# A gated delta-rule layer with experts on one core: the first inverse level begins its banks, and three VectorE instructions of each item go to ScalarE and GpSimd

## The chip, the cores and the metric

The kernel runs on one core of one Trainium2 chip. The metric is the device time of one execution, in microseconds. A core has TensorE (matrix products, in the rows PE, its weight loads PEld), VectorE (DVE), ScalarE (ACT), GpSimd (POOL) and SyncE (SP), which issues the DMAs. Each engine works through its own list of instructions in order; semaphores tie the lists together.

## The reference, cut to what matters

One layer over 2 sequences of 2048 tokens with 256 features: a gated delta-rule attention (16 value heads and 8 key heads of 128), and behind it a mixture of 16 experts. The part that the change touches:

```python
mixed = hidden_states @ Wqkv.T + bqkv          # then a causal convolution of 4 taps along the tokens, and silu
q = _l2norm(q) * DK ** (-0.5); k = _l2norm(k)   # _l2norm(x) = x * rsqrt(sum(x * x) + 1e-6)
def step(state, inp):                           # for every token
    state = state * jnp.exp(g_t)[..., None, None]
    delta = (v_t - jnp.einsum('bhk,bhkv->bhv', k_t, state)) * b_t[..., None]
    state = state + k_t[..., None] * delta[:, :, None, :]
    out = jnp.einsum('bhk,bhkv->bhv', q_t, state)
var = jnp.mean(core * core, axis=-1, keepdims=True)
core = core * lax.rsqrt(var + RMS_EPS) * norm_w * jax.nn.silu(zg)
```

## The kernel before

The tokens are cut into 32 chunks of 128, and the 16 value heads into 4 groups of 4. One **item** is one group g of one chunk t; g is also called its slot. The recurrence inside a chunk is solved in matrix form, which needs the inverse of a 128x128 unit triangular matrix for each head. GpSimd inverts the 16x16 blocks on the diagonal (`base_inverse`); SyncE takes the triangle `Ln` to DRAM and the blocks back, and then the block inverses to DRAM and into the full tiles `XiT` and `Xi`. TensorE then doubles the block size in three levels.

The work is pipelined over items by hand. In each engine's `item(w, stages)` five items are in flight: `a` (three ahead: projection, convolution taps, gate), `f` (two ahead: norms, exponents, the triangle), `v` (one ahead: the inverse levels), `w` (the state's recurrence) and `u` (one behind: output projection). The order of calls in `item` is the order on the engine; nothing else decides it. The experts of chunk t-1 and the front of chunk t+1 are laid in at fixed slots.

A level n of the inverse is: TensorE `invert_q` (L554: bQ = LnR applied to XiT), VectorE `mask_q` (L1191: Qi = bQ times the level's 0/1 mask), TensorE `invert_xt` (L562, into bank bXT) and `invert_x` (L567, into bank bX), ScalarE `inverse_t` and `inverse` (L934 and L941, which copy the banks back to XiT and Xi). The banks accumulate: `invert_begin` first puts XiT and Xi themselves into them by a product with the identity (L544, L545), and each level adds its correction. After the third level TensorE turns XiT (`turned`, L573), forms the residual (L580, L582), and in the next item corrects Xi (`correct`, L589), which VectorE copies to Tt (`refined`, L1207). Tt is what the state's solve (L611) multiplies with.

Other lines that the steps touch:
- TensorE: `kkq` and `exponents` (L526 to L530, with bf16 products), `ss` (L501: row sums of the squares of q and k, it waits for ScalarE's Sq, L880), `z_proj` (L484, L486).
- VectorE: `taps` (L1148), `tails_out` (L1162, needs Bk and Hd), `first_tokens` (L1172), `squares` (L1183 makes Sse = sum + epsilon, L1185 makes Epq from it), `ended` (L1154 makes Bk, the bias of the rows that end a sequence), `out_norm` (L1237 sums ScalarE's squares of O along the row into Ss, L1239 makes Vv), `gate_bias` (L1201).
- ScalarE: `square_o` (L959, squares O into CoT), `activated` (a table load, three Silus, a table load, Sq), `key_norm` (L897), `out_norm` (L963, L965), `norm` (L975, L977), `decays` (L925, makes Ex).
- GpSimd: `exponents` (HG and Parts), `before_first` (L1495 to L1501, makes Hd), `decay_keys` (Kd), `minus_l` and `attention` (L1481), `base_inverse` (L1577 to L1604).

Of the kernel before, what the change touches and what calls it, by code (L numbers as in the profile page):

```python
# [35 lines left out]
ALU = mybir.AluOpType  # L36
# [3 lines left out]
P = 128  # L40
# [29 lines left out]
def constants(chunks, chunks_of_batch):  # L70
# [8 lines left out]
    for n in range(LEVELS):  # L79
        b = r >> (LO + n)  # L80
        f[:, C_LEVEL + n * P:C_LEVEL + (n + 1) * P] = (b[:, None] % 2 == 1) & (b[None, :] == b[:, None] - 1)
    last = np.arange(chunks) % chunks_of_batch == chunks_of_batch - 1
# [18 lines left out]
def layer_kernel(nc, x, wqkv, conv, wz, wba, rows, cols, wout, shared1, wlat, shared2, wup, rw, rw2,  # L101
# [6 lines left out]
    with ctx:  # L108
# [64 lines left out]
        Sse = sb("Sse", [P, 2 * GK])  # L173
        Epq = sb("Epq", [P, GROUPS, GK])
# [70 lines left out]
        def heads(bank):  # L245
# [12 lines left out]
            xt_done=LEVELS, sq_done=1, lnr_done=1, oq_done=1,  # L258

            bk_done=1, tails_done=2, convqk_done=TAPS, convv_done=TAPS, sse_done=1, epq_done=1, kkq_done=1, hg_done=4, parts_done=5,  # L260
            q_done=LEVELS + 1, tt_done=1, r_done=2, o_done=2, s_done=2, so_done=1, vv_done=1, core_done=1, acc_done=1,

            h_done=5, neg_done=1, at_done=1, kd_done=2, base_done=BASE_STEPS,
# [187 lines left out]
        def _(pe):  # L451
# [81 lines left out]
            def invert_begin(v, front):  # L533
                f = ahead(v, 1)
                if front:
                    pe.wait_ge(sem["partsT_done"], at("partsT_done", f))
                    pe.wait_ge(sem["vs_done"], at("vs_done", f))
                    pe.wait_ge(sem["ex_done"], at("ex_done", f))
                else:
                    pe.wait_ge(sem["xt_done"], at("xt_done", ahead(v, -1)))  # L540
                    pe.wait_ge(sem["tt_done"], at("tt_done", ahead(v, -1)))
                    pe.wait_ge(sem["q_done"], at("q_done", ahead(v, -1)))
                pe.wait_ge(sem["xb_in"], at("xb_in", v))
                mm(bXT[:, :], IdR[:, 0, :], XiT[:, :, :], start=True, stop=True)  # L544
                mm(bX[:, :], IdR[:, 0, :], Xi[:, :, :], start=True, stop=True)  # L545

            def invert_q(v, n):
                if n == 0:
                    pe.wait_ge(sem["lnr_done"], at("lnr_done", v))
                else:  # L550
                    pe.wait_ge(sem["xt_done"], at("xt_done", v, n))
                    pe.wait_ge(sem["q_done"], at("q_done", v, n))
                for h in range(GH):
                    last = mm(heads(bQ)[:, h, :], LnR[:, h, :], XiT[:, h, :], start=True, stop=True)  # L554
                last.then_inc(sem["q_full"], 1)

            def invert_xt(v, n):
# [1120 lines left out]
```

## Time and profile before

| what | value |
|---|---|
| median of 3 runs | 3390.93 us (3383.54 to 3395.1) |
| the profiled execution | 3389.08 us, its span 3387.3 us |
| granted TensorE clock, mean | 0.988 |
| TensorE busy | 3222.1 us, 95% |
| its weight loads | 2861.1 us, 84% |
| VectorE busy | 2720.6 us, 80% |
| ScalarE busy | 2412.1 us, 71% |
| GpSimd busy | 2140.9 us, 63% |
| DMA | 15.8% of 16 engines' span |

The busy share of every engine is the same in each fortieth of the span but the first and the last, so one chunk stands for all. In the chunk that the rows below are from, slot 0 starts at 1516.78 us, slot 1 at 1540.63, slot 2 at 1568.20 and slot 3 at 1594.17, by the first product of the state (L603) on TensorE. A timeline merges equal instructions that follow one another: its second column then runs from the first one's start to the last one's end. TensorE's ends are modelled, and a product is recorded as longer than the distance to the next one's start, so its price in the stream is read from start to start.

### The profile page before, as it was taken

What the parts mean: (1) busy time and instruction counts of PE and PEld (TensorE: products, weight loads), DVE (VectorE), ACT (ScalarE), POOL (GpSimd) and SP (SyncE); (2) the same over time, 40 slices, a digit from 0 to 9 for tenths busy, and PEclk for the clock granted to TensorE, in tenths of its full rate; (3) what the DMA queues carried; (4) which work ended last, traced back from release to release, by engine and by line L of the source; (5) the groups of instructions that cost most, each with busy time, mean ns of one, the idle gap of its engine ahead of it and who ended that gap; (6) DMA issues with size and microseconds to landing.
All of it is one profiled execution on the core that took longest, in us unless ns stands there. A gap on an engine that the chain in (4) does not pass through costs nothing.

```text
span 3387.3 us, 77356 instructions
## 1 busy us (share of the span) xinstructions
PE 3222.1 (95%) x24096; PEld 2861.1 (84%) x24096; DVE 2720.6 (80%) x8720; ACT 2412.1 (71%) x5922; POOL 2140.9 (63%) x5380
## 2 busy tenths in 40 slices
PE   4999999999999999999999999999999999999996
PEld 3888888888888888888888888888888888888885
DVE  4788888888888888888888878888888888888874
ACT  3777777777777777777777777777777777777762
POOL 2766666666666666666666666666666666666660
PEclk8999999999999999999999999999999999999997
DMA  4111111111111111111111111111111111111110
GB/s 181 36 46 38 37 44 38 38 44 41 36 43 40 38 44 41 36 40 42 37 39 47 36 35 45 40 38 44 40 34 45 41 37 45 39 34 43 43 36 11
DMA packets 424114, 144.77 MB, mean 43 GB/s; under 512 B 211168, under 2 KB 421664, under 8 KB 423200
## 3 DMA queue, kind: packets, MB, share of 16 engines
q1 hardware_dynamic: 423712, 139.83, 15.8%
q8 instruction: 201, 3.29, 0.4%
q14 instruction: 201, 1.65, 0.2%
HBM read 93.11 MB, written 46.66 MB: 41 GB/s over the span
## 4 chain that ended last, share of the span: by engine, by line
PE 64%; ACT 12%; DVE 9%; issue 8%; POOL 4%; DMA 3%; SPq 0%; DVEq 0%; ACTq 0%; POOLq 0%
PE bF L473 8%; PE bB L644 6%; PE bQ L554 4%; ACT L847 4%; PE bS L611 3%; PE bXT L562 3%; PE bB L729 3%; PE bB L716 3%; PE bXT L501 2%; PE bS L619 2%; PE bD L626 2%; PE bQ L493 2%; PE bS L603 2%; PE bF L484 2%; PE bD L604 2%
## 5 line engine op out<-in xcount | busy, mean ns | idle before, releaser
L1148 DVE SCALAR_TENSOR_TENSOR Y<-bF,Cv,Y 128x127 f32<-128x127 f32 (+2 forms) x3072 | 850.8, 338 | 7.2 <-ACT Y L864 2.4
L473 PE MATMUL bF<-XnT,Wqkv 128*128 128x128 f32 x4096 | 533.5, 278 | 0.5 <-ACT XnT L983 0.5
L473 PEld LDWEIGHTS bF<-XnT,Wqkv 128*128 128x128 f32 x4096 | 507.0, 194 | 9.5 <-issue 2.1
L864 ACT ACTIVATE Y<-bF,Cv 128x128 f32<-128x128 f32 x1024 | 382.6, 454 | 102.1 <-PE bF L473 102.1
L934 ACT ACTIVATE XiT<-bXT 128x512 fp32r<-128x512 f32 x384 | 228.7, 596 | 307.2 <-PE bXT L562 302.4
L1587 POOL TENSOR_TENSOR Tp<-Tp 32x64 f32<-32x64 f32 (+2 forms) x768 | 360.0, 469 | 60.2
L1191 DVE TENSOR_TENSOR Qi<-bQ,Cf 128x512 fp32r<-128x512 f32 x384 | 263.6, 686 | 99.2 <-PE bQ L554 97.8
L847 ACT ACT_TABLE_LOAD x257 | 329.7, 1283 | 5.3 <-PEq L1671 0.7
L562 PE MATMUL bXT<-Qi,Xi 128*128 128x128 f32 x1536 | 302.5, 320 | 2.3 <-DVE Qi L1191 2.3
L562 PEld LDWEIGHTS bXT<-Qi,Xi 128*128 128x128 f32 x1536 | 222.6, 192 | 96.4 <-DVE Qi L1191 46.3
L1580 POOL TENSOR_TENSOR Tp<-Yb,Tm 32x64 f32<-32x64 f32 (+1 forms) x384 | 276.6, 720 | 30.1
L1580 POOL TENSOR_TENSOR Tp<-Cb,Yb 32x64 f32<-32x64 f32 (+1 forms) x384 | 274.0, 713 | 30.1
L1595 POOL TENSOR_TENSOR Yb<-Cb,Cf 32x8 fp32r<-32x8 f32 x128 | 25.7, 201 | 410.8 <-DMA Cb<-DL 410.8
L554 PE MATMUL bQ<-XiT,LnR 128*128 128x128 f32 x1536 | 240.9, 280 | 19.4 <-ACT XiT L934 19.4
L554 PEld LDWEIGHTS bQ<-XiT,LnR 128*128 128x128 f32 x1536 | 211.9, 191 | 47.9 <-ACT XiT L934 28.8
L644 PE MATMUL bB<-Wout,CoT 128*128 128x256 f32 x1024 | 244.2, 382 | 0.9 <-ACT CoT L970 0.8
L1481 POOL TENSOR_TENSOR Ln<-Ex,KKQ 128x512 f32<-128x512 f32 x128 | 163.7, 1279 | 127.4 <-issue 123.3
L941 ACT ACTIVATE Xi<-bX 128x512 fp32r<-128x512 f32 x384 | 226.4, 590 | 2.8 <-PE bX L573 2.3
L1514 POOL TENSOR_TENSOR HG<-LnbG,Lnk 128x4 f32<-128x4 f32 x128 | 25.9, 202 | 316.1 <-ACT Lnk L897 316.1
L644 PEld LDWEIGHTS bB<-Wout,CoT 128*128 128x128 f32 x1024 | 185.9, 192 | 21.6 <-ACT CoT L970 1.1
L1183 DVE TENSOR_SCALAR Sse<-bXT 128x4 f32<-128x4 f32 x128 | 20.3, 159 | 191.3 <-PE bXT L501 191.3
L1017 ACT ACTIVATE Rl<-bB 128x512 f32<-128x512 f32 x124 | 74.1, 597 | 139.1 <-PE bF L717 139.1
(236 smaller groups left out, 9507.5 us busy)
## 6 DMA issues: line engine op xcount, KB each, us to landing
DL<-Ln SPq DMA_DIRECT2D x128, 256.0 KB, 2.2
XiT<-DX SPq DMA_DIRECT2D x128, 256.0 KB, 2.8
Xi<-DX SPq DMA_DIRECT2D x128, 256.0 KB, 3.2
DX<-Yb SPq DMA_DIRECT2D x256, 32.0 KB, 1.9
Xf<-x SPq DMA_DIRECT2D x32, 128.0 KB, 3.0
Wqkv<-wqkv SPq DMA_DIRECT2D x4, 1024.0 KB, 17.0
Cb<-DL SPq DMA_DIRECT2D x128, 32.0 KB, 1.9
Xr<-x SPq DMA_DIRECT2D x32, 128.0 KB, 3.3
```

What stands on the lines that cost most here:

```text
L473: last = mm(bank[:, i, :], Wqkv[:, k, c:c + P], XnT[:, k, :], start=(k == 0), stop=(k == KT - 1))
L554: last = mm(heads(bQ)[:, h, :], LnR[:, h, :], XiT[:, h, :], start=True, stop=True)
L562: last = mm(heads(bXT)[:, h, :], Xi[:, h, :], Qi[:, h, :], start=False, stop=True, skip_group_check=True)
L644: last = mm(bB[:, 0:HID], CoT[:, h, :], Wout[:, g * GH + h, :], start=(h == 0), stop=(h == GH - 1))
L847: nc.scalar.add_instruction(mybir.InstLoadActFuncSet(name=nc.get_next_instruction_name(), act_func_set_id=TABLES[name], engine=mybir.Engin ...
L864: last = op(Y[:, tile, :], bank[:, i, :], ACT.Identity, scale=c[:, TAPS - 1:TAPS], bias=c[:, TAPS:TAPS + 1])
L934: op(XiT[:, :, :], heads(bXT), ACT.Copy).then_inc(sem["xt_done"], 1)
L941: op(Xi[:, :, :], heads(bX), ACT.Copy).then_inc(sem["xi_done"], 1)
L1148: last = stt(y, bank[:, i, 0:P - shift], Cv[:, g * TILES + tile, n:n + 1], y, ALU.mult, ALU.add)
L1191: tt(Qi[:, :, :], heads(bQ), level, ALU.mult).then_inc(sem["q_done"], 1)
L1580: then(tt(view(Tp[:, :], p * m ** 3, [[m * m, m], [m, m], [1, m]]), pair(left, p), pair(right, p), ALU.mult))
L1587: then(tt(lo, lo, hi, ALU.add))
```

## The change

- The first level of the inverse begins the banks. The mask of level 0 gets the identity added, TensorE puts an identity into bank bQ (one bf16 product of 512 columns) and adds LnR applied to XiT to it, so that the masked Qi is identity plus correction, and the level's product alone gives the whole new XiT and Xi. The two 512-column products of `invert_begin` are gone. Of its waits, those for the banks bXT and bX move to `invert_xt` and `invert_x` of level 0, those for bank bQ and for the loaded blocks stay ahead of the identity product.
- ScalarE squares O head by head (four 128x128 instructions instead of one 128x512), each with its sum along the row written to Ss by `accum_out`; VectorE's reduction L1237 is gone.
- Epq is gone: Sse is kept for each group, Vv is made from it with another factor, and the epsilon comes in as the scale of ScalarE's logarithm.
- Bk is made by GpSimd in `before_first`, ahead of Hd, with a wait for the tails of the item before; VectorE's `ended` is gone.

```diff
@@ -79,6 +79,7 @@
         f[:, C_LEVEL + n * P:C_LEVEL + (n + 1) * P] = (b[:, None] % 2 == 1) & (b[None, :] == b[:, None] - 1)
+    f[:, C_LEVEL:C_LEVEL + P] += np.eye(P)
     last = np.arange(chunks) % chunks_of_batch == chunks_of_batch - 1
@@ -170,8 +171,7 @@
         Sq = sb("Sq", [P, 2 * GK, P])
-        Sse = sb("Sse", [P, 2 * GK])
-        Epq = sb("Epq", [P, GROUPS, GK])
+        Sse = sb("Sse", [P, GROUPS, 2 * GK])
         Lnk = sb("Lnk", [P, GK])
@@ -530,41 +530,44 @@
 
-            def invert_begin(v, front):
-                f = ahead(v, 1)
-                if front:
-                    pe.wait_ge(sem["partsT_done"], at("partsT_done", f))
-                    pe.wait_ge(sem["vs_done"], at("vs_done", f))
-                    pe.wait_ge(sem["ex_done"], at("ex_done", f))
-                else:
-                    pe.wait_ge(sem["xt_done"], at("xt_done", ahead(v, -1)))
-                    pe.wait_ge(sem["tt_done"], at("tt_done", ahead(v, -1)))
-                    pe.wait_ge(sem["q_done"], at("q_done", ahead(v, -1)))
-                pe.wait_ge(sem["xb_in"], at("xb_in", v))
-                mm(bXT[:, :], IdR[:, 0, :], XiT[:, :, :], start=True, stop=True)
-                mm(bX[:, :], IdR[:, 0, :], Xi[:, :, :], start=True, stop=True)
-
-            def invert_q(v, n):
+            def invert_q(v, n, front=None):
                 if n == 0:
+                    if front:
+                        pe.wait_ge(sem["ex_done"], at("ex_done", ahead(v, 1)))
+                    else:
+                        pe.wait_ge(sem["q_done"], at("q_done", ahead(v, -1)))
+                    pe.wait_ge(sem["xb_in"], at("xb_in", v))
+                    mm(bQ[:, :], identb, identb.unsqueeze(1).to_broadcast([P, GH, P]), start=True, stop=True)
                     pe.wait_ge(sem["lnr_done"], at("lnr_done", v))
...
                 for h in range(GH):
-                    last = mm(heads(bQ)[:, h, :], LnR[:, h, :], XiT[:, h, :], start=True, stop=True)
+                    last = mm(heads(bQ)[:, h, :], LnR[:, h, :], XiT[:, h, :], start=(n > 0), stop=True,
+                                  skip_group_check=True)
                 last.then_inc(sem["q_full"], 1)
 
-            def invert_xt(v, n):
+            def invert_xt(v, n, front=None):
+                if n == 0 and front:
+                    pe.wait_ge(sem["partsT_done"], at("partsT_done", ahead(v, 1)))
+                elif n == 0:
+                    pe.wait_ge(sem["xt_done"], at("xt_done", ahead(v, -1)))
                 pe.wait_ge(sem["q_done"], at("q_done", v, n + 1))
...
                 for h in range(GH):
-                    last = mm(heads(bXT)[:, h, :], Xi[:, h, :], Qi[:, h, :], start=False, stop=True, skip_group_check=True)
+                    last = mm(heads(bXT)[:, h, :], Xi[:, h, :], Qi[:, h, :], start=(n == 0 and h == 0), stop=True,
+                              skip_group_check=True)
                 last.then_inc(sem["xt_full"], 1)
 
-            def invert_x(v, n):
+            def invert_x(v, n, front=None):
+                if n == 0 and front:
+                    pe.wait_ge(sem["vs_done"], at("vs_done", ahead(v, 1)))
+                elif n == 0:
+                    pe.wait_ge(sem["tt_done"], at("tt_done", ahead(v, -1)))
                 for h in range(GH):
-                    last = mm(heads(bX)[:, h, :], Qi[:, h, :], Xi[:, h, :], start=False, stop=True, skip_group_check=True)
+                    last = mm(heads(bX)[:, h, :], Qi[:, h, :], Xi[:, h, :], start=(n == 0 and h == 0), stop=True,
+                                  skip_group_check=True)
                 last.then_inc(sem["x_full"], 1)
@@ -775,8 +778,7 @@
                 if invert:
-                    invert_begin(v, front)
-                    invert_q(v, 0)
+                    invert_q(v, 0, front)
                 if c and g == 1:
@@ -784,8 +786,8 @@
                 if invert:
-                    invert_xt(v, 0)
-                    invert_x(v, 0)
+                    invert_xt(v, 0, front)
+                    invert_x(v, 0, front)
                 if e and g == 3:
@@ -894,7 +896,7 @@
                 act.wait_ge(sem["hg_done"], at("hg_done", ahead(f, -1)))
-                op(Lnk[:, :], Sse[:, 1:2 * GK:2], ACT.Ln).then_inc(sem["lnk_done"], 1)
+                op(Lnk[:, :], Sse[:, f[1], 1:2 * GK:2], ACT.Ln).then_inc(sem["lnk_done"], 1)
                 act.wait_ge(sem["lnk_done"], at("lnk_done", f))
@@ -954,13 +956,15 @@
                 act.wait_ge(sem["o_done"], at("o_done", w))
-                act.wait_ge(sem["so_done"], at("so_done", ahead(w, -1)))
+                act.wait_ge(sem["vv_done"], at("vv_done", ahead(w, -1)))
                 act.wait_ge(sem["po_full"], at("po_full", ahead(w, -1)))
-                op(CoT[:, :, :], O[:, :, :], ACT.Square).then_inc(sem["oq_done"], 1)
+                for h in range(GH):
+                    last = op(CoT[:, h, :], O[:, h, :], ACT.Square, accum_out=Ss[:, h:h + 1])
+                last.then_inc(sem["so_done"], 1)
 
...
                 act.wait_ge(sem["vv_done"], at("vv_done", w))
-                op(Vl[:, :], Vv[:, :], ACT.Ln).then_inc(sem["lnf_done"], 1)
+                op(Vl[:, :], Vv[:, :], ACT.Ln, scale=RMS_EPS * P).then_inc(sem["lnf_done"], 1)
                 act.wait_ge(sem["lnf_done"], at("lnf_done", w))
@@ -1148,12 +1152,6 @@
 
-            def ended(f):
-                t, g = f
-                dve.wait_ge(sem["tails_done"], at("tails_done", ahead(f, -1)))
-                ts(Bk[:, :].unsqueeze(2), Cv[:, g * TILES:(g + 1) * TILES, TAPS + 1:TAPS + 2],
-                   Cf[:, LAST:LAST + chunks].unsqueeze(2)[:, t, :], None, ALU.mult).then_inc(sem["bk_done"], 1)
-
             def tails_out(f, half):
@@ -1180,9 +1178,7 @@
                 dve.wait_ge(sem["lnk_done"], at("lnk_done", ahead(f, -1)))
-                ts(Sse[:, :], bXT[:, 0:2 * GK], L2_EPS, None, ALU.add).then_inc(sem["sse_done"], 1)
-                dve.wait_ge(sem["sse_done"], at("sse_done", f))
-                ts(Epq[:, f[1], :], Sse[:, 0:2 * GK:2], RMS_EPS * P, None, ALU.mult).then_inc(sem["epq_done"], 1)
+                ts(Sse[:, f[1], :], bXT[:, 0:2 * GK], L2_EPS, None, ALU.add).then_inc(sem["sse_done"], 1)
 
@@ -1233,11 +1229,9 @@
                 t, g = w
-                dve.wait_ge(sem["oq_done"], at("oq_done", w))
-                nc.vector.tensor_reduce(Ss[:, :], CoT[:, :, :], AX.X, ALU.add).then_inc(sem["so_done"], 1)
                 dve.wait_ge(sem["so_done"], at("so_done", w))
-                stt(Vv[:, :].rearrange("p (a b) -> p a b", a=GK), Ss[:, :].rearrange("p (a b) -> p a b", a=GK), 1.0 / P,
-                    Epq[:, g, :].unsqueeze(2).to_broadcast([P, GK, GH // GK]), ALU.mult, ALU.add).then_inc(sem["vv_done"], 1)
+                stt(Vv[:, :].rearrange("p (a b) -> p a b", a=GK), Ss[:, :].rearrange("p (a b) -> p a b", a=GK), 1.0 / (P * RMS_EPS * P),
+                    Sse[:, g, 0:2 * GK:2].unsqueeze(2).to_broadcast([P, GK, GH // GK]), ALU.mult, ALU.add).then_inc(sem["vv_done"], 1)
 
@@ -1380,8 +1374,6 @@
                     squares(f)
-                if new:
-                    ended(a)
                 if state:
@@ -1489,7 +1481,9 @@
                 wide = lambda n, k: c[:, :, n:n + 1].to_broadcast([P, TILES, k])
-                pool.wait_ge(sem["tails_done"], at("tails_done", (t - 1, g)))
+                pool.wait_ge(sem["tails_done"], at("tails_done", ahead(f, -1)))
+                tt(Bk[:, :], c[:, :, TAPS + 1:TAPS + 2].rearrange("p a b -> p (a b)"),
+                   Cf[:, LAST:LAST + chunks].unsqueeze(2)[:, t, :].to_broadcast([P, TILES]), ALU.mult).then_inc(sem["bk_done"], 1)
                 pool.wait_ge(sem["convqk_done"], at("convqk_done", ahead(f, -1)))
```

## Rows read from the trace of the kernel before

**Rows 1.** The page's chain of work that ended last, by engine
```profile
PE 64%; ACT 12%; DVE 9%; issue 8%; POOL 4%; DMA 3%; SPq 0%; DVEq 0%; ACTq 0%; POOLq 0%
```

**Rows 2.** Timeline of TensorE, slot 2: start us, length us, line, out<-in
```profile
1576.07 0.38 PE L526 MATMUL bQ<-Ch 128*128 128x512 bf16 x1
1576.29 0.39 PE L528 MATMUL bQ<-PartsT,Ch 128*128 128x128 bf16 x4
...
1578.43 0.48 PE L544 MATMUL bXT<-XiT,IdR 128*128 128x512 f32 x1
1578.75 0.40 PE L545 MATMUL bX<-Xi,IdR 128*128 128x512 f32 x1
1578.98 0.56 PE L554 MATMUL bQ<-XiT,LnR 128*128 128x128 f32 x4
...
1580.32 0.66 PE L562 MATMUL bXT<-Qi,Xi 128*128 128x128 f32 x4
```

**Rows 3.** Timeline of VectorE, slot 2, up to the first mask
```profile
1579.36 0.23 DVE L1162 SCALAR_TENSOR_TENSOR Tails<-bF,Cf,Bk 128x12 f32<-128x12 f32 x1
1579.58 0.69 DVE L1191 TENSOR_TENSOR Qi<-bQ,Cf 128x512 fp32r<-128x512 f32 x1
```

**Rows 4.** Timeline of VectorE, slot 0
```profile
1521.56 0.15 DVE L1183 TENSOR_SCALAR Sse<-bXT 128x4 f32<-128x4 f32 x1
...
1521.95 0.68 DVE L1207 COPY Tt<-bX 128x512 f32<-128x512 f32 x1
```

**Rows 5.** Timeline of TensorE, slot 0 (the window ends inside the group)
```profile
1522.69 0.49 PE L611 MATMUL bS<-R,Tt 128*128 128x128 f32 x2
```

**Rows 6.** Timeline of ScalarE, end of slot 0 (square, copy) and slot 1 (Sq)
```profile
1537.80 0.61 ACT L959 ACTIVATE CoT<-O 128x512 f32<-128x512 f32 x1
1538.32 0.58 ACT L934 ACTIVATE XiT<-bXT 128x512 fp32r<-128x512 f32 x1
...
1543.46 0.63 ACT L880 ACTIVATE Sq<-QK 128x512 f32<-128x512 f32 x1
```

**Rows 7.** Timeline of ScalarE, slots 1 and 2: small instructions and their steps
```profile
1556.51 0.32 ACT L1006 ACTIVATE Rg<-Rg 128x128 f32<-128x128 f32 x1
1556.72 0.60 ACT L934 ACTIVATE XiT<-bXT 128x512 fp32r<-128x512 f32 x1
...
1575.56 0.20 ACT L907 ACTIVATE Sc<-HG 128x4 f32<-128x4 f32 x1
1575.66 0.20 ACT L908 ACTIVATE Sc<-HG 128x8 f32<-128x8 f32 x1
```

**Rows 8.** Timeline of TensorE, slots 0 and 1, with idle time and its end
```profile
1538.95 0.66 PE L573 MATMUL bX<-IdR,XiT 128*128 128x128 f32 x4 [0.80 <-ACT XiT L934]
...
1544.24 1.02 PE L501 MATMUL bXT<-Cf,Sq 128*128 128x1 f32 x8 [0.35 <-ACT Sq L880]
```

**Rows 9.** Timeline of ScalarE, end of slot 2 and slot 3 (Sq)
```profile
1590.27 0.61 ACT L959 ACTIVATE CoT<-O 128x512 f32<-128x512 f32 x1
1590.99 0.60 ACT L934 ACTIVATE XiT<-bXT 128x512 fp32r<-128x512 f32 x1
...
1595.88 0.63 ACT L880 ACTIVATE Sq<-QK 128x512 f32<-128x512 f32 x1
```

**Rows 10.** Timeline of TensorE, slots 2 and 3: the products that wait for Sq
```profile
1571.30 1.02 PE L501 MATMUL bXT<-Cf,Sq 128*128 128x1 f32 x8 [0.23 <-ACT Sq L880]
...
1596.81 0.95 PE L501 MATMUL bXT<-Cf,Sq 128*128 128x1 f32 x8
```

**Rows 11.** Timeline of ScalarE, slot 3 of the chunk before
```profile
1513.38 0.60 ACT L934 ACTIVATE XiT<-bXT 128x512 fp32r<-128x512 f32 x1 [0.96 <-PE bXT L562]
```

**Rows 12.** The page's groups: busy us, mean ns, idle us before and its end
```profile
L1481 POOL TENSOR_TENSOR Ln<-Ex,KKQ 128x512 f32<-128x512 f32 x128 | 163.7, 1279 | 127.4 <-issue 123.3
```

**Rows 13.** Timeline of VectorE, slot 1
```profile
1561.85 1.21 DVE L1172 TENSOR_TENSOR Y<-Y,Hd 128x12 f32<-128x12 f32 x1
```

**Rows 14.** Timeline of GpSimd, slot 1
```profile
1561.55 1.48 POOL L1580 TENSOR_TENSOR Tp<-Cb,Yb 32x512 f32<-32x512 f32 x1
```

More of the change, by code:

```diff
@@ L257, in layer_kernel @@
             kn_done=1, vs_done=1, xi_done=LEVELS, qg_done=2, z_done=2, lnf_done=1, fr_done=1, coT_done=1,
-            xt_done=LEVELS, sq_done=1, lnr_done=1, oq_done=1,
-            bk_done=1, tails_done=2, convqk_done=TAPS, convv_done=TAPS, sse_done=1, epq_done=1, kkq_done=1, hg_done=4, parts_done=5,
+            xt_done=LEVELS, sq_done=1, lnr_done=1,
+            tails_done=2, convqk_done=TAPS, convv_done=TAPS, sse_done=1, kkq_done=1, hg_done=4, parts_done=5,
             q_done=LEVELS + 1, tt_done=1, r_done=2, o_done=2, s_done=2, so_done=1, vv_done=1, core_done=1, acc_done=1,
-            h_done=5, neg_done=1, at_done=1, kd_done=2, base_done=BASE_STEPS,
+            h_done=5, bk_done=1, neg_done=1, at_done=1, kd_done=2, base_done=BASE_STEPS,
             ln_out=16, lc_in=16, xs_out=32, xs_seen=1, xb_in=32,
```

## The prediction

> **What bounds the kernel now.** I read four views, in this order: the chain of work that ended last, TensorE's own timeline over one chunk, then ScalarE's and VectorE's timelines beside it, and the waits of each instruction that TensorE waits for. The chain says that TensorE holds 64% of the span, ScalarE 12% and VectorE 9% [rows 1]: the kernel is a TensorE stream, in a fixed order, that is handed over to ScalarE or VectorE at a few points in each item and back. So an edit counts only where it sits on TensorE between two such points, or on another engine at one of them. Slots 0 to 3 are the four items of a chunk (g = 0 to 3); all timeline rows but that of group 11 lie in one steady chunk, and I count 31 such chunks.
>
> **Part 1, the bank-beginning level (TensorE).** Removed in each item are the two 512-column identity products L544 and L545; start to start they take 0.32 and 0.23 us. Added is one bf16 product of 512 columns, which is the form of L526: 0.22 us from its start to the next [rows 2]. That saves 0.55 - 0.22 = 0.33 us by starts; if the first product is worth no more than the second (0.23, the rest being a start that is drawn forward behind the f32 products), 0.46 - 0.22 = 0.24. I take 0.25 and keep 0.33.
>
> Does it reach the end? The next handover on TensorE is the first L562, which waits for the mask Qi. In slot 2 the mask ends at 1579.58 + 0.69 = 1580.27 and L562 starts at 1580.32 [rows 2, 3], so TensorE already waits for VectorE there, and it is the same 0.05 us in slots 0 and 3. The mask in turn starts as the Tails update ends (1579.36 + 0.23) [rows 3], at the end of an unbroken run of VectorE work that begins with the update of S after TensorE's new-state products, ahead of the saved ones. The product it masks will be there sooner, so it can start only the overlap of two VectorE instructions sooner, some 0.1 us. Of 0.25 us, 0.1 arrives in slots 0, 2 and 3; the rest becomes waiting. In slot 1 the shared expert's products stand between, and 0.25 passes. The waits that moved from the removed block (partsT_done, vs_done) are now later in TensorE's order and their signals come before it: no cost.
>
> **Part 2, VectorE sheds.** Gone are the row reduction of the squares, Epq and Bk. Epq and Bk stand between Sse and the copy Tt, and Tt is what TensorE's solve waits for in slot 0: Sse ends at 1521.56 + 0.15 = 1521.71 and Tt starts at 1521.95 [rows 4]; L611 starts at 1522.69, 0.05 after Tt ends [rows 5]. Tt can start as Sse ends, with that overlap: 0.27 us come off, in slot 0. In the other slots Tt waits for TensorE's correction anyway, so nothing. The reduction stands behind the gate's bias, and what follows (Vv, the last mask) is needed only in the middle of the next item: it is time saved off the path, and I cost it at nothing. So VectorE loses three instructions in each item, and 0.27 us in one item of four is all that arrives.
>
> **Part 3, ScalarE takes the row sums.** One 128x512 Square becomes four 128x128 ones, each with a sum. The old one holds ScalarE for 1538.32 - 1537.80 = 0.52 us [rows 6]. A 128x128 Square from SBUF holds it for 0.21 us (1556.51 to 1556.72) [rows 7]. What the sum itself costs no row of this trace shows. If it is free: 4 x 0.21 - 0.52 = 0.32 us more. If it is an extra tiny instruction, the nearest rows are Sc's: 0.10 us from start to start, 0.20 us long each [rows 7]. With steps: 4 x (0.21 + 0.10) - 0.52 = 0.72. If neither overlaps (0.32 + 0.20 for each head): 1.56. A gain is excluded, since four fixed starts replace one. I take 0.72, since a sum that is kept in the engine has to be written out, and independent small instructions here do overlap. The Trainium skill (ScalarE: Activation LUTs, What ACT_TABLE_LOAD costs) has 186 ns plus 0.833 ns a column for an ACTIVATE and about 93 ns of overlap; that is an estimate of 0.20 us a head, the trace's 0.21 agrees, and by that price alone, with a free sum, the extension would be 0.28 us.
>
> Where does the 0.72 lie? Behind the square in ScalarE's order stand the copy XiT of the third level, two table loads, three Silus and Sq, and TensorE waits for XiT and for Sq.
> - Slot 0: the square starts only when the norm's ScalarE steps are over, XiT follows it without a gap, and TensorE's L573 starts 0.05 us after XiT with 0.80 us of waiting behind it; L501 waits for Sq, 0.15 us after its end [rows 6, 8]. No cover: +0.72. Net of 0.27 and 0.1: +0.35.
> - Slot 2: the square ends at 1590.88, XiT starts at 1590.99: cover 0.11 us. Sq ends at 1596.51 in slot 3 [rows 9], and L501 starts at 1596.81 with no idle before it [rows 10]; it needs 0.15 of that 0.30, so 0.15 more is cover. +0.72 - 0.26 = +0.46, less the 0.1 of part 1: +0.36.
> - Slot 1: the same small gap as in slot 2 (0.1 us), so XiT, for which TensorE waits there, comes 0.72 - 0.1 - 0.25 = 0.37 us later; but L501 of the next item has 0.23 us of idle time ahead of it [rows 10], on a chain that comes through VectorE's late gate bias and not through XiT. +0.14.
> - Slot 3: ScalarE idles 0.96 us ahead of that XiT [rows 11]: covered. Only the 0.1 of part 1: -0.1.
>
> **Part 4, GpSimd and the logarithm.** Bk becomes one 128x8 GpSimd instruction of some 0.2 us ahead of Hd. It delays the queue behind it (Hd, Kd, then Ln), but ahead of Ln's 128 instructions GpSimd idles 127.4 us, 1 us each [rows 12]; of the waits in the code ahead of Ln, the one for Ex is the late one, and that eats it; without that cover it would be 0.2 us in each item at GpSimd's rate. Its new wait (tails_done of the group before) is older than the conv waits behind it. The epsilon as a scale in the Ln changes no count. Cost nothing.
>
> **Sum.** 0.35 + 0.14 + 0.36 - 0.1 = +0.75 us a chunk, x 31 = 23 us. The profiled execution took 3389.08 us (span 3387.3), close to the median of three, 3390.93. Forecast 3389 + 23 = 3412 us, +0.7%. With a free sum (0.32) the slots give -0.05, 0, -0.04 and -0.1: 3383 us. With 1.56: 1.19, 0.98, 1.20 and 0.5: +3.9 us a chunk, 3509 us.
>
> **Rivals.**
> A, cheap sum: the extension stays near 0.3 us, cover takes half of it, and the saved products pay for the rest. 3378 to 3398, most likely 3385. For it: the engine sums while it streams. Against: the sums must reach Ss somehow.
> B, the port comes free (faster). In slot 1 the 12-column add L1172 lasts 1.21 us for its 12 columns and ends as a 1.48 us GpSimd product ends, which had begun 0.30 us before it [rows 13, 14]. GpSimd's time hangs on Ex, ahead of the saved products. If VectorE comes 0.25 to 0.33 us sooner, it can slip in ahead of that product. The Trainium skill (SBUF — State Buffer, Who interferes with whom) says so: a VectorE instruction with two SBUF inputs and a GpSimd one that reads SBUF exclude each other, and whoever starts first keeps the pair; the rows agree, and by that rule this item would gain. The gain is bounded by what stands beside: the 0.23 us of idle ahead of L501, and ScalarE's own extension. With a dear sum it is swallowed (3410); with a cheap one it gives slot 1 -0.3 us, a chunk -0.5, and 3374 us.
> C, the sum is dear, each read-out waiting for its Square: 1.1 to 1.6 us more. With 1.1 the slots give 0.73, 0.52, 0.74 and 0.04, +2.0 us a chunk: 3452 to 3509. It decides from 0.96 us on, where slot 3 loses its cover too.
> D, the masks don't bind, and all of 0.25 to 0.33 passes in all slots: 0.15 to 0.23 us more off in three slots, 0.45 to 0.7 us a chunk: 3390 to 3398. Against it stands the 0.05 us in three slots.
>
> **How the numbers follow.** Forecast case (extension 0.6 to 0.95 us, 3401 to 3434) 0.48; A 0.20; B with a cheap sum 0.08; C 0.12; D 0.12. The range leaves out the far half of C and the edges: 3374 to 3456. About 0.3% (10 us) is what a measurement of this kernel can tell from no change. Slower by more: the forecast and C, 0.60. Within: most of A and D, 0.27. Faster by more: B and the edge of A, 0.13.
>
> **What would show it.** In the profile after: four Squares of about 0.3 us for each item, and whether 0.10 us or more stands between them; L573 of slot 0 waiting about 0.7 us longer, L501 of slot 3 now idle ahead by about 0.4; the wait of the first L562 for Qi grown by 0.15 us in slots 0, 2 and 3 (part 1 right) or not (D); L611 of slot 0 free of Tt; L1172 of slot 1 at 1.2 us (forecast) or 0.2 (B); VectorE less busy while the span does not follow. A Square step of 0.21 us would make the forecast wrong, and so would a ScalarE that idles ahead of XiT in slot 0.

## The result, and the profile after

The changed kernel takes 3419.11 us (median, 3417.98 to 3420.43), the kernel before 3389.05 us beside it: a ratio of 1.0091, 95% interval 1.0078 to 1.0104. It is slower by 30 us. The forecast was 3412 us.

The page of the kernel after: first engines' busy time, then the chain of work that ended last.

```profile
PE 3213.4 (94%) x23968; PEld 2839.2 (83%) x23968; DVE 2603.8 (76%) x8336; ACT 2490.9 (73%) x6818; POOL 2168.9 (63%) x5508
```
```profile
PE 47%; ACT 16%; POOL 14%; issue 12%; DVE 5%; DMA 5%; SPq 0%; POOLq 0%; DVEq 0%; ACTq 0%
```

TensorE lost 9 us of work and VectorE 117 us; ScalarE gained 79 us, and the span is 28.9 us longer. So what matters is where on ScalarE the 79 us lie, not that the sum over the engines fell. The chain differs from [rows 1] by more than the time does: GpSimd's share rose from 4% to 14%. The experiments below show what that share is worth.

One chunk, cut at the first product of the state in each slot, shows where the time came (mean of 28 chunks, us): slot 0 +0.69, slot 1 +0.20, slot 2 -0.16, slot 3 +0.36, together +1.09. Over 31 chunks that is 34 us, 5 more than the span grew; the rest lies in the chunks at the ends, which I didn't follow.

**ScalarE's sums.** Timeline of ScalarE after, end of slot 0 (start us, length us, line, out<-in):

```profile
1547.43 0.29 ACT L962 ACTIVATE CoT<-O 128x128 f32<-128x128 f32 x1
1547.63 0.19 ACT L962 ACTIVATION_READ_ACCUMULATOR CoT<-O 128x1 f32 x1
1547.72 0.29 ACT L962 ACTIVATE CoT<-O 128x128 f32<-128x128 f32 x1
...
1548.60 0.57 ACT L936 ACTIVATE XiT<-bXT 128x512 fp32r<-128x512 f32 x1
```

Each sum is an instruction of its own behind its Square. From start to start, Square to read-out is 0.20 us and read-out to the next Square 0.09, so a head takes 0.29 us and four take 1.17, where the one Square took 0.52 [rows 6]: ScalarE's chain is 0.65 us longer. TensorE pays it where it waits for XiT in slot 0, and for Sq in slot 3 (timelines of TensorE and ScalarE after; in brackets the idle time ahead and what ended it):

```profile
1549.22 0.66 PE L576 MATMUL bX<-IdR,XiT 128*128 128x128 f32 x4 [1.44 <-ACT XiT L936]
```
```profile
1607.62 1.02 PE L501 MATMUL bXT<-Cf,Sq 128*128 128x1 f32 x8 [0.19 <-ACT Sq L882]
```
```profile
1606.85 0.63 ACT L882 ACTIVATE Sq<-QK 128x512 f32<-128x512 f32 x1
```

The first idle time was 0.80 us [rows 8], the second was nothing [rows 10]. The bracket of the second tells half of it: L501 starts 3.00 us into slot 3 (at 1607.62, the slot at 1604.62), where before it started 2.64 us in (1596.81, the slot at 1594.17), so by starts it comes 0.36 us later, the whole of what slot 3 grew by.

**The level.** Timelines of TensorE and of VectorE after, slot 0:

```profile
1537.17 0.38 PE L540 MATMUL bQ<-Ch 128*128 128x512 bf16 x1
1537.20 0.74 PE L546 MATMUL bQ<-XiT,LnR 128*128 128x128 f32 x4
1537.78 0.65 PE L606 MATMUL bS<-S,QK 128*128 128x256 f32 x2
...
1538.98 0.63 PE L559 MATMUL bXT<-Qi,Xi 128*128 128x128 f32 x4
```
```profile
1538.02 0.22 DVE L1160 SCALAR_TENSOR_TENSOR Tails<-bF,Cf,Bk 128x12 f32<-128x12 f32 x1
1538.16 0.68 DVE L1187 TENSOR_TENSOR Qi<-bQ,Cf 128x512 fp32r<-128x512 f32 x1
```

TensorE reaches the state's products 0.25 us sooner, as taken. Then it waits for the mask: from the second of the state's products (L607, before L604) to the level's first one (L559, before L562) it now takes 0.72 us, before 0.46 (means over the chunks, the same in slots 0, 2 and 3), so the wait eats all of it up to that product.

**Parts.** In slot 0 TensorE now waits where it never waited before, for GpSimd (timeline of TensorE after):

```profile
1533.70 0.22 PE L514 MATMUL bXT<-Ch,Parts 128*128 128x128 bf16 x1 [0.17 <-POOL Parts L1521]
```

### The profile page after: what moved, and what is told of

Its sections match the earlier page's. It is cut to its first block, busy times and chain, and to the rows that moved or that the text cites. A ratio compares the mean times of both kernels' runs of the same rounds, so it can differ in the third digit from the quotient of the medians.

```text
span 3416.2 us, 77738 instructions
## 1 busy us (share of the span) xinstructions
PE 3213.4 (94%) x23968; PEld 2839.2 (83%) x23968; DVE 2603.8 (76%) x8336; ACT 2490.9 (73%) x6818; POOL 2168.9 (63%) x5508
## 4 chain that ended last, share of the span: by engine, by line
PE 47%; ACT 16%; POOL 14%; issue 12%; DVE 5%; DMA 5%; SPq 0%; POOLq 0%; DVEq 0%; ACTq 0%
PE bF L473 6%; PE bB L647 5%; POOL Tp L1574 4%; ACT L849 4%; PE bQ L546 3%; ACT CoT L962 3%; POOL Tp L1581 3%; PE bXT L501 3%; ACT XiT L936 2%; DMA DL<-Ln 2%; PE bS L614 2%; PE bB L719 2%; PE bXT L559 2%; DMA Cb<-DL 2%; PE bS L606 2%
## 5 line engine op out<-in xcount | busy, mean ns | idle before, releaser
L559 PEld LDWEIGHTS bXT<-Qi,Xi 128*128 128x128 f32 x1536 | 222.7, 192 | 117.4 <-issue 88.1
L559 PE MATMUL bXT<-Qi,Xi 128*128 128x128 f32 x1536 | 300.0, 318 | 13.9 <-DVE Qi L1187 2.3
L546 PE MATMUL bQ<-XiT,LnR 128*128 128x128 f32 x1536 | 264.5, 295 | 19.5 <-ACT XiT L936 19.5
L962 ACT ACTIVATE CoT<-O 128x128 f32<-128x128 f32 x512 | 150.7, 295 | 55.7 <-DVE O L1219 55.7
```

Of the source, the lines that this page charges most:

```text
L559: last = mm(heads(bXT)[:, h, :], Xi[:, h, :], Qi[:, h, :], start=(n == 0 and h == 0), stop=True, skip_group_check=True)
L962: last = op(CoT[:, h, :], O[:, h, :], ACT.Square, accum_out=Ss[:, h:h + 1])
```

## The experiments

The theory after these traces: the kernel is a TensorE stream that is late where ScalarE, VectorE or GpSimd hand over late; the sums cost 1.1 us a chunk, the level gives little since the mask binds, and Epq's and Bk's gain is lost on GpSimd's Parts. Rival U: the chain's 14% for GpSimd is the cause. Rival V: the level itself costs. L, S and K name the three parts: the level, the row sums on ScalarE, and Epq gone with Bk on GpSimd. The table has all runs: the ratio to the kernel before with its interval, and by how much each slot is longer than before (us, mean of 28 chunks of the profiled execution). The chunks of one execution agree well in slots 0 and 3 (standard error of a mean 0.02 us or less) and less well in slots 1 and 2 (up to 0.06 us, 0.14 in slot 1 and 0.08 in slot 2 of e11), so differences of a tenth there are not clear. The kernel before was measured anew beside each group of experiments (medians 3386.3 to 3389.1 us), so runs of different groups are compared by their ratios.

| run | parts | median us | ratio (95%) | slots 0, 1, 2, 3 | chunk |
|---|---|---|---|---|---|
| changed kernel | L S K | 3419.11 | 1.0091 (1.0078-1.0104) | +.69 +.20 -.16 +.36 | +1.09 |
| e1_sums_on_dve | L K | 3384.48 | 0.9992 (0.9983-1.0001) | +.03 -.19 +.09 -.06 | -0.13 |
| e2_only_level | L | 3380.63 | 0.9982 (0.9973-0.9992) | -.03 -.13 +.10 -.06 | -0.12 |
| e3_only_sums_act | S | 3422.56 | 1.0099 (1.0083-1.0114) | +.61 +.37 -.20 +.37 | +1.15 |
| e4_only_bk_epq | K | 3389.70 | 1.0008 (0.9999-1.0017) | +.07 -.11 +.09 -.02 | +0.03 |
| e6_after_old_level | S K | 3424.02 | 1.0102 (1.0087-1.0118) | +.70 +.31 -.19 +.38 | +1.19 |
| e5_four_squares_dve_sum | L K, half of S | 3392.97 | 1.0024 (1.0015-1.0033) | +.30 -.16 +.12 +.01 | +0.27 |
| e7_halves | L S K, moved | 3386.86 | 1.0004 (0.9995-1.0012) | +.08 -.17 +.20 -.06 | +0.06 |
| e9_level_early_mask | L K, moved | 3373.96 | 0.9967 (0.9954-0.9980) | -.09 -.13 +.10 -.19 | -0.30 |
| e10_halves_early_mask | L S K, both moved | 3380.89 | 0.9981 (0.9972-0.9990) | -.04 -.15 +.20 -.18 | -0.17 |
| e11_only_level_early_mask | L, moved | 3376.77 | 0.9964 (0.9950-0.9977) | -.12 +.09 +.09 -.16 | -0.11 |
| e12_bk_epq_products_first | K, moved | 3386.72 | 0.9992 (0.9983-1.0001) | 0 -.12 +.11 -.03 | -0.04 |
| e13_all_moves | L K, moved twice | 3373.93 | 0.9957 (0.9943-0.9971) | -.10 -.16 +.09 -.19 | -0.35 |

### The parts alone, and one taken back

e1 takes the sums out of the changed kernel:

```diff
-                for h in range(GH):
-                    last = op(CoT[:, h, :], O[:, h, :], ACT.Square, accum_out=Ss[:, h:h + 1])
-                last.then_inc(sem["so_done"], 1)
+                op(CoT[:, :, :], O[:, :, :], ACT.Square).then_inc(sem["oq_done"], 1)
...
+                dve.wait_ge(sem["oq_done"], at("oq_done", w))
+                nc.vector.tensor_reduce(Ss[:, :], CoT[:, :, :], AX.X, ALU.add).then_inc(sem["so_done"], 1)
```

> The changed kernel with its row sums put back: ScalarE makes the four heads' squares of O in one instruction and VectorE reduces them, as before the change; the level that begins the bank and GpSimd's making of Bk stay. Theory (the path through slot 0 and ScalarE's extension): the 0.65 us that ScalarE's sum chain is longer by per item goes, so a chunk loses about 0.65 us in slot 0, 0.3 in slot 1 and 0.4 in slots 2 and 3, and what is left of the change is the level's saving: 3372 to 3385 us, a ratio of 0.995 to 0.999 against the kernel before. Rival U (GpSimd's longer work and its DMAs are what lengthened the kernel): the time stays at 3405 to 3420 us, since GpSimd does here all it does in the changed kernel. Rival V (the level itself costs, by its first q product and the mask that it now waits for): 3395 to 3405 us.

e2, e3 and e4 are the kernel before with one of the change's own pieces each (the pieces of the diff ahead of the prediction).

> The kernel before with one part of the change: the first level begins its bank (the identity product and the bf16 product's place changed as in the change); row sums, Epq and Bk as before. Theory: 0.25 us of TensorE an item is saved, of which 0.2 or more is given back to the wait for VectorE's mask in slots 0, 2 and 3, so 0.3 to 0.6 us a chunk stay: 3372 to 3382 us. Rival V (the level costs): 3392 to 3400 us. If the masks did not bind, 1.0 us a chunk would stay: 3358 us.

> The kernel before with one part of the change: the row sums are made by ScalarE's accumulator, four squares an item; the level, Epq and Bk as before. Theory: ScalarE's chain is longer by 0.65 us an item and nothing is gained for it: +0.65 us in slot 0, +0.3 in slot 1, 0.4 in slot 2 and 0 to 0.4 in slot 3, some 1.3 to 1.7 us a chunk: 3430 to 3442 us. Rival U (GpSimd is the cause, the sums are hidden): 3389 to 3400 us.

> The kernel before with one part of the change: Epq is gone from VectorE and Bk is made by GpSimd; the level and the row sums as before. Theory: VectorE's Tt in slot 0 starts 0.3 us sooner, but GpSimd's Parts come 0.1 to 0.2 us later because VectorE's gate operations on two SBUF inputs now lie on them, so the gain is lost: 3386 to 3394 us. Rival U (GpSimd's longer work lengthens the kernel): 3405 to 3420 us. If the 0.27 us a chunk of the prediction did arrive: 3381 us.

Alone, the sums cost 0.99% (34 us, less than the 41 to 53 expected), the level gives 0.18%, and Epq with Bk cost 0.08%, which the interval doesn't tell from nothing. The three add up to +0.89%, the whole change measured +0.91%. So the sums are the cause, and U falls: e4 and e1 do all of GpSimd's new work, and neither can be told from the kernel before. This is e4's chain:

```profile
PE 49%; POOL 14%; issue 12%; ACT 11%; DVE 8%; DMA 5%; SPq 0%; POOLq 0%; ACTq 0%; DVEq 0%
```

It shows the same 14% for GpSimd at the time of the kernel before, and e3, as slow as the changed kernel, shows 3%. The share has a real wait behind it: GpSimd has 14% in the eight kernels in which TensorE waits for Parts in slot 0 (0.17 us in the mean), and 2 to 4% in the six in which it doesn't. From the transpose of Parts the chain of e4 runs back through the exponents and `base_inverse` on GpSimd for 10 us (1515.35 to 1525.91), where before it runs from L611 back through Tt. But all that the wait adds to TensorE's time there is 0.1 us: the share names a place, and its size isn't a cost. V falls with e2.

e6 takes only the level back from the changed kernel:

> The changed kernel with its level put back: row sums on ScalarE, Epq gone and GpSimd's Bk stay. Theory (the parts add up: sums +36, Bk and Epq +3, level -6): 3422 to 3430 us. Rival (the level gives nothing while the sums hold ScalarE back): 3415 to 3421 us.

3424.02 us: by the ratios the level would be worth 0.1% with the sums on ScalarE too, but the intervals of e6 and of the changed kernel overlap, so this run alone doesn't show it. It fits e2's 0.18%.

### What of the sum costs, and where it could stand

e5 splits the Square without the accumulator; VectorE reduces:

```diff
-                    last = op(CoT[:, h, :], O[:, h, :], ACT.Square, accum_out=Ss[:, h:h + 1])
+                    last = op(CoT[:, h, :], O[:, h, :], ACT.Square)
```

> The changed kernel with half of the new row sum: ScalarE squares the four heads of O one by one, but without its accumulator, and VectorE reduces them as before the change. It measures what of ScalarE's 0.65 us longer chain is the split into four instructions and what the read-out of the accumulator. Theory (the steps in the trace: 0.199 us from a square to its read-out, 0.092 from the read-out to the next square): four squares at 0.20 us against one at 0.52 us, so the chain is longer by 0.28 us and not 0.65, and of the 35 us that the sums cost some 15 remain: 3396 to 3404 us. Rival S1 (the split is the whole price, reading out is hidden): 3413 to 3421 us. Rival S2 (the read-outs, recorded at 186 ns each, are the whole price): 3381 to 3387 us.

Timelines of ScalarE, end of slot 0, of e1 and of e5:

```profile
1533.60 0.61 ACT L961 ACTIVATE CoT<-O 128x512 f32<-128x512 f32 x1
1534.12 0.58 ACT L936 ACTIVATE XiT<-bXT 128x512 fp32r<-128x512 f32 x1
```
```profile
1541.12 0.89 ACT L962 ACTIVATE CoT<-O 128x128 f32<-128x128 f32 x4
1541.91 0.57 ACT L936 ACTIVATE XiT<-bXT 128x512 fp32r<-128x512 f32 x1
```

From the first Square to XiT it is 0.52 us in e1, 0.79 in e5 and 1.17 in the changed kernel: 0.27 us for the split, 0.38 for the four read-outs, as expected. The time was missed on the low side (3392.97 for 3396 to 3404), since the price isn't in proportion. Against e1, e5's 0.27 us cost +.27, +.02, +.03 and +.07 us in the four slots, the 0.65 us of the changed kernel +.66, +.38, -.25 and +.41. Slot 0 pays all of either; ahead of slot 3's wait for Sq about 0.24 us of cover swallow nearly all of the 0.27 and less than half of the 0.65.

e7 makes two of the four sums earlier, where ScalarE idles behind the decays, and keeps all of the change. Its squares go to a buffer of their own, Sd, and so the wait for po_full, which guards CoT, is gone too; that this wait cost nothing was not tried by itself. The calls, cut:

```diff
                     decays(f)
+                if state:
+                    square_o(w, 0)        # heads 0 and 1, waits for o_done(w, 1)
...
                 if state:
-                    square_o(w)
+                    square_o(w, 1)        # heads 2 and 3
```

> The changed kernel with the same work in another place: ScalarE makes the sums of heads 0 and 1 earlier, in its idle time of about 1 us behind the decays of the next item, and those of heads 2 and 3 where all four stood; the squares are dumped in a buffer of their own. Theory (the cost of the sums is the place of 4 x 0.29 us in ScalarE's chain and not their amount): only 2 x 0.29 - 0.52 = 0.06 us of the extension is left, so the 32 us that the change cost are mostly back: 3384 to 3394 us. Rival W (the first half isn't covered: O's first two heads are ready too late, or the last tap behind it is on the path): 3402 to 3425 us.

Timeline of ScalarE in e7, end of slot 0:

```profile
1532.13 0.29 ACT L963 ACTIVATE Sd<-O 128x128 f32<-128x128 f32 x1
...
1532.71 0.57 ACT L937 ACTIVATE XiT<-bXT 128x512 fp32r<-128x512 f32 x1
```

0.58 us from the first late Square to XiT, for 0.52 of the single one, and 3386.86 us, a ratio of 1.0004 for 1.0091: some 29 us come back with the same instructions, in another place. ScalarE is even busier than in the changed kernel (2509.5 us for 2490.9). This is the run that shows most directly that the cost was the place in ScalarE's order and not ScalarE's 79 us.

### The mask that takes the level's saving

e9 moves one call of VectorE in e1:

```diff
                     taps(a, 0, 0)
+                if invert and g != 1:
+                    mask_q(v, 0)
+                if new:
                     tails_out(a, 0)
```

> The kernel e1_sums_on_dve (the level and GpSimd's Bk, row sums on VectorE) with one step of VectorE moved: in slots 0, 2 and 3 the mask on q of the first level runs ahead of the 0.23 us copy of the tails, not behind it. It asks whether that mask is what gives the level's saving back: in the run of the level alone TensorE passed 0.255 us sooner and lost 0.22 to 0.26 us at the wait for the mask. Theory: three slots a chunk gain 0.2 us each, 0.6 x 31 = 19 us: 3362 to 3370 us. Rival X (the next wait, of ScalarE's or VectorE's chain behind, takes it back, or the later tails cost as much): 3380 to 3388 us.

Timelines of VectorE and TensorE in e9, slot 0:

```profile
1519.30 0.68 DVE L1185 TENSOR_TENSOR Qi<-bQ,Cf 128x512 fp32r<-128x512 f32 x1
1519.89 0.22 DVE L1158 SCALAR_TENSOR_TENSOR Tails<-bF,Cf,Bk 128x12 f32<-128x12 f32 x1
```
```profile
1520.12 0.63 PE L559 MATMUL bXT<-Qi,Xi 128*128 128x128 f32 x4
```

The level's product comes 0.13 to 0.15 us sooner in all three slots: the mask did bind. I had expected 0.2: Tails is 0.22 us long, but from its start to the next one's only 0.14 (1538.02 to 1538.16 above). Slots 0 and 3 keep it. Slot 2 loses it again, half a slot later (VectorE, GpSimd and TensorE in e9, slot 2):

```profile
1579.32 1.19 DVE L1168 TENSOR_TENSOR Y<-Y,Hd 128x12 f32<-128x12 f32 x1
```
```profile
1578.98 1.49 POOL L1577 TENSOR_TENSOR Tp<-Cb,Yb 32x512 f32<-32x512 f32 x1
```
```profile
1580.56 0.70 PE L484 MATMUL bF<-Wz,XnT 128*128 128x512 f32 x1 [0.20 <-DVE Y L1168]
```

The 12-column add ends with GpSimd's product. It lasts 1.24 us in e9 and 1.06 in e1 (means of 28): the sooner VectorE gets there, the longer it stands. GpSimd's product hangs on its own chain and didn't move. So two slots of three gain, 0.25 us a chunk, 8 of the 19 us expected (3373.96 for 3362 to 3370); by the ratios e9 is some 8 us faster than e1.

> Both moves together on the changed kernel, all three parts of the change kept: the sums in two halves and the mask ahead of the tails. Theory: the two are independent, so the 19 us of the earlier mask come on top of what the halves give: 3365 to 3375 us. Rival: with VectorE freed of the reduction the masks are early already, and the move adds nothing to the halves: 3384 to 3394 us.

e10 stands between the two cases (3380.89 us, for 3365 to 3375 if all adds up and 3384 to 3394 if nothing does): its slots 0 and 3 are each 0.12 us shorter than e7's, slot 2 is not, as in e9. The moves are independent; it was the same slot 2 that I had counted.

### Why Epq and Bk gave nothing

Timelines of GpSimd (HG and Parts), slot 0, before and in e4:

```profile
1522.30 0.20 POOL L1518 TENSOR_TENSOR Parts<-HG,Cf 128x8 bf16<-128x8 f32 x1
1522.46 0.20 POOL L1519 TENSOR_TENSOR HG<-HG 128x4 f32<-128x4 f32 x1
1522.62 0.34 POOL L1521 TENSOR_TENSOR HGf<-HG,Parts 128x8 f32<-128x8 f32 x1
```
```profile
1524.21 0.32 POOL L1509 TENSOR_TENSOR Parts<-HG,Cf 128x8 bf16<-128x8 f32 x1
1524.50 0.30 POOL L1510 TENSOR_TENSOR HG<-HG 128x4 f32<-128x4 f32 x1
1524.75 0.31 POOL L1512 TENSOR_TENSOR HGf<-HG,Parts 128x8 f32<-128x8 f32 x1
...
1525.70 0.20 POOL L1518 TENSOR_TENSOR Parts<-HGf,Cf 128x8 bf16<-128x8 f32 x1
```

VectorE's gate operations behind Tt, before and in e4:

```profile
1522.55 1.13 DVE L1249 SCALAR_TENSOR_TENSOR O<-O,Fr,Gz 128x128 f32<-128x128 f32 x4
```
```profile
1524.13 1.13 DVE L1240 SCALAR_TENSOR_TENSOR O<-O,Fr,Gz 128x128 f32<-128x128 f32 x4
```

They read O and Gz, two sources in SBUF. Four with steps of 0.26 us (1.13 - 0.34 over three), each 0.34 long: in e4 they end at 1524.47, 1524.73 and 1524.99, and the three GpSimd instructions, each begun about 0.1 us behind one, end at 1524.53, 1524.80 and 1525.06, every time 0.06 us later. Before, gates began 0.33 us later in the slot: only the third one was caught (it ends at 1522.96, the gate over it at 1522.89), and an instruction that began ahead of a gate (L1519) took its 0.20 us. With the gates drawn forward by Epq's and Bk's absence, Parts come 0.20 us later, TensorE waits for them, and it is 0.1 us behind before it goes on. By the means of the chunks, counted from the slot's start, e4's products behind Tt (L610) come at 5.60 us for 5.90 before, as predicted, the transpose of Parts at 7.35 for 7.34, and the transposes of V two steps behind it (L519, before L520) at 7.94 for 7.84. TensorE before and in e4 (the slots start at 1516.78 and 1518.70):

```profile
1524.13 0.22 PE L514 MATMUL bXT<-Ch,Parts 128*128 128x128 bf16 x1
```
```profile
1524.31 0.68 PE L610 MATMUL bS<-R,Tt 128*128 128x128 f32 x4
...
1526.05 0.22 PE L513 MATMUL bXT<-Ch,Parts 128*128 128x128 bf16 x1 [0.17 <-POOL Parts L1518]
```

The Trainium skill (SBUF — State Buffer, Who interferes with whom) has this as a rule: a VectorE instruction with two SBUF inputs excludes a GpSimd one that reads SBUF, and the one that issued first keeps the shared ports. The ends 0.06 us apart agree with it.

e12 moves the gates in e4, and nothing else:

```diff
+                if front and g == 0:
+                    products(f)
                 if post:
                     gated(u)
-                if front:
+                if front and g != 0:
                     products(f)
```

> The kernel e4_only_bk_epq with one step of VectorE moved: in slot 0 the products of k with k and q (source in PSUM) run ahead of the four gate operations on O (two sources in SBUF), not behind them. In e4 TensorE's work behind Tt begins 0.3 us sooner than in the kernel before, but then waits for GpSimd's Parts, whose first three operations are 0.32, 0.30 and 0.31 us there, against 0.20, 0.20 and 0.34 before; each begins about 0.1 us behind the start of a gate operation. Theory (those gates are why the 0.27 us of the prediction did not arrive): with the gates 0.6 us later the first three are 0.20, 0.20 and at most 0.34 us, Parts end at most 0.1 us later than in the kernel before, and slot 0 is 0.1 to 0.3 us shorter than in e4: 3379 to 3387 us. Rival Y (the gates fall on the operations behind, and Parts come as late as in e4, or the transpose of O now waits for the gates): 3388 to 3396 us.

Timelines of GpSimd and of TensorE in e12, slot 0:

```profile
1522.16 0.20 POOL L1511 TENSOR_TENSOR Parts<-HG,Cf 128x8 bf16<-128x8 f32 x1
1522.33 0.20 POOL L1512 TENSOR_TENSOR HG<-HG 128x4 f32<-128x4 f32 x1
1522.48 0.20 POOL L1514 TENSOR_TENSOR HGf<-HG,Parts 128x8 f32<-128x8 f32 x1
```
```profile
1523.77 0.23 PE L513 MATMUL bXT<-Ch,Parts 128*128 128x128 bf16 x1
1524.03 0.66 PE L632 MATMUL bB<-Cf,O 128*128 128x128 f32 x4
```

All three take 0.20 us, with VectorE's products, which read one source in SBUF and one in PSUM, beside them (1522.24 to 1522.93), and TensorE comes to the transpose of the parts 0.23 us sooner than before: this is where the predicted 0.27 arrives. Then the transpose of O (L632) waits for the last gate, which ends at 1523.98, 0.05 us ahead of it; it comes 0.26 us behind the transpose of the parts instead of 0.06, and the slot is as long as before the change. That wait for the gates is what rival Y had named; slot 0 is 0.07 us shorter than in e4, for 0.1 to 0.3 expected. By the ratios 5 us lie between e4 and e12, and the intervals just overlap, so the times don't tell the two apart; the traces carry the verdict. The step's gain exists only up to the next handover, and in that stretch two of them (Parts and the gates) compete for it.

> The kernel e9_level_early_mask (level, GpSimd's Bk, sums on VectorE, mask ahead of the tails) with the products of slot 0 ahead of the gates as well. If the two moves are independent it stands to e9 as e12 to e4: 3362 to 3372 us; if Rival Y holds, 3374 to 3382 us.

> The kernel e2_only_level with the mask ahead of the tails in slots 0, 2 and 3: of the change the level alone, Epq, Bk and the row sums as before. Theory (the parts add up: Bk and Epq cost 2 to 4 us whatever the rest): 2 to 4 us less than e9_level_early_mask, 3368 to 3373 us. Rival (with the mask early, GpSimd's Bk costs nothing): 3373 to 3377 us.

e13 and e9 can't be told apart (their intervals overlap, the slots differ by 0.03 us at most), and e13 lies outside the 3362 to 3372 us expected if the two moves added up: whether the second one gives anything there is inconclusive. e11's time lies in the range of the rival case, and its ratio can't be told from e9's: with the mask early, no cost and no gain of Epq and Bk can be seen. Its chunk is 0.19 us longer than e9's, all of it in slot 1, where single chunks of e11 lie up to 3 us above the others. e9 and e13 beat both kernels, by 0.3 to 0.4% against before and 1.2 to 1.3% against the changed one.

## Why the prediction was right, point by point

- **The sign and its reason**: right. The sums alone are +0.99%, everything else together is -0.08% (e1), which its interval doesn't tell from nothing.
- **Extension of ScalarE, 0.72 us**: 0.65 measured. The form was right (a small instruction of its own behind each Square), the split costs 0.27 and the read-outs 0.38. Neither bound (0.32, 1.56) is near. Rivals A and C fall.
- **Slot 0, +0.35**: wrong, +0.69. The extension arrived nearly whole (+0.61 alone, of 0.65), but of the two gains set against it neither did. Part 2's -0.27 measured +0.07: the step that failed says that Tt can start sooner, which it did (0.33 us, and TensorE's L611 0.30 us), and stops there. I looked at what waits for Tt, not at what stands behind Tt on VectorE (the gates, two SBUF sources) and runs beside GpSimd's chain. Rival B's own mechanism, two engines on shared ports, was at work here, and I had looked for it in slot 1 alone.
- **The level, 0.25 us**: saved as computed. Alone (e2), of the 0.1 that should arrive in slots 0, 2 and 3, slot 0 got 0.03, slot 3 0.06 and slot 2 nothing (+0.10 there, in a slot that scatters); of the 0.25 that should pass in slot 1, 0.13 is seen, and that slot scatters too. The mask did end 0.09 us sooner in slot 0 (e2), as taken. But TensorE's product now begins 0.15 us behind the mask's end, in slots 0, 2 and 3 of every kernel with the level, and 0.05 in every one without it [rows 2, 3]. So the step that fails in slots 0 and 3 is "the waits that moved: no cost", or something else in the new form of the level. What speaks for the waits: the product of old had one wait, the new one has two, the late one (q_done) behind partsT_done, as L501 has, which also begins 0.15 us behind Sq [rows 6, 8]; L573 with one wait begins 0.05 behind XiT, and L611, whose late wait is the first of its two, 0.05 behind Tt [rows 4, 5]. Three more places fit: the transpose of Parts (late wait second) begins 0.15 us behind Parts where it waits for them, in slot 1 before the change too; L554 of the later levels and, in e12, the transpose of O (late wait first) begin 0.05 to 0.07 us behind. That is argued from seven places; changing the order of the two waits was not tried, and it stays open. Rival D falls: e9 gained by moving the mask.
- **Slots 1 and 2 up to the end of slot 2**: +0.14 less 0.1, so +0.04; measured +0.04, and that the two agree is luck. L573 of slot 1 comes 0.20 us later in its slot where 0.37 was forecast, since the extension is 0.65 us and the gap ahead of XiT was 0.20 us in that slot (0.72 us from the Square to XiT before, in the mean), and not the 0.1 taken over from slot 2. The slack ahead of the next Sq then gives 0.22 us back, as argued (0.23). The rest of slot 2 is 0.06 us longer, where part 1 should have made it 0.1 shorter. Two misses of 0.17 and 0.16 us cancel.
- **Slot 3, where slot 2's extension arrives**: +0.46 less 0.1, so +0.36; measured +0.36. The cover of 0.26 us from [rows 9, 10] measured 0.24, so 0.41 arrived, and the level gave about half of its 0.1: here too two small misses cancel.
- **Rival B**: not seen. In slot 1 the 12-column add lasts 1.06 us on average after and 0.93 before. My rows 13 and 14 showed one chunk, and I took it for all: in 7 of the 28 chunks of either kernel it takes less than 0.3 us, mostly the 0.17 us of an add that comes ahead of GpSimd's product. It is a race that each chunk decides anew. The add came only 0.1 us sooner in its slot, not the 0.25 to 0.33 that the rival asked for, and that doesn't turn it.
- **The sum**, +0.75 us a chunk, was +1.09; the 0.34 between them is slot 0, and nearly all of it part 2's step. The time came 7 us from the forecast. By the chunks it would be 10 us (0.34 x 31); the ends of the kernel, which nobody followed, make up the difference.

## What to carry to other kernels

A sum made by ScalarE's accumulator is a second instruction for each row group, so work moved there must be priced from start to start with its read-out, and then placed: the same four sums cost 34 us at the end of a chain that TensorE waits for, and some 4 us (e7 against e1, within their intervals) when two of them stand half a slot earlier, in a stretch where ScalarE idles. When an edit lets an engine start sooner, follow not only who waits for that instruction but what comes behind it on the same engine, and which other engine it will now run beside. The chain that ended last can move by 10% of the span between two kernels of the same time, for a wait that delays TensorE by 0.1 us: take a share in it as a place to look, and find the cost by an experiment that does that part alone.

## What the runs showed of the hardware

- `accum_out` on ScalarE is issued as a Square and an ACTIVATION_READ_ACCUMULATOR: 0.20 us to the read-out, 0.09 us from it to the next Square; a head of 128x128 takes 0.29 us against 0.20 without it (changed kernel and e5).
- A GpSimd instruction of 0.20 us that begins under a VectorE one with two SBUF sources ends 0.06 us after it: begun within 0.12 us of it, 0.20 became 0.30 to 0.34 (e4, and the kernel before). One that begins ahead of it is not slowed.
- The other way round, a VectorE add of 12 columns that begins under a GpSimd product of 1.49 us ends with it, mostly 1.0 to 1.5 us for 0.17 us of work. Timelines of VectorE and GpSimd after, slot 1, in a chunk where it came first:

```profile
1572.01 0.17 DVE L1170 TENSOR_TENSOR Y<-Y,Hd 128x12 f32<-128x12 f32 x1
```
```profile
1572.21 1.50 POOL L1574 TENSOR_TENSOR Tp<-Cb,Yb 32x512 f32<-32x512 f32 x1
```
